# First node pass of a graph network: one inverse root for two norms, normalised rows written by ScalarE

## The reference, cut to what matters

```python
def _layernorm(x, axis=-1, eps=1e-05):
    m = jnp.mean(x, axis=axis, keepdims=True)
    v = jnp.var(x, axis=axis, keepdims=True)
    return (x - m) / jnp.sqrt(v + eps)
...
h = x @ w_in + b_in                                   # x is _layernorm of the input
...
xn = _layernorm(h, ln1_g[l], ln1_b[l])                # l = 0
q = (xn @ wq[l] + bq[l]).reshape(n, H, DH)
k = (xn @ wk[l] + bk[l]).reshape(n, H, DH)
v = (xn @ wv[l] + bv[l]).reshape(n, H, DH)
```

## Time and profile before

| what | us |
|---|---|
| median of 3 runs | 4462.18 |
| lowest and highest run | 4457.46, 4467.36 |
| span of the profiled execution, from its first to its last instruction | 4465.3 |
| TensorE busy in it | 3681.2 (82%) |
| VectorE busy in it | 3232.5 (72%) |
| ScalarE busy in it | 1681.1 (38%) |
| POOL busy in it | 2072.2 (46%) |

### The profile page before, as it was taken

How to read it: one execution, slowest core, us unless ns; L and a number is a source line. 1 busy time by engine, 2 the same in 40 slices (tenths; PEclk the granted TensorE clock), 3 DMA queues, 4 the chain that set the end, 5 groups by cost and what they waited for, 6 DMA issues and landing times. The chain is left out here.

```text
span 4465.3 us, 82525 instructions
## 1 busy us (share of the span) xinstructions
PE 3681.2 (82%) x17048; PEld 2435.5 (55%) x17048; DVE 3232.5 (72%) x7299; ACT 1681.1 (38%) x4755; POOL 2072.2 (46%) x1938
## 2 busy tenths in 40 slices
PE   1777898888998857999988888888888758888488
PEld 1444555555555535777765555455555437777377
DVE  4777899888998865555548998898899766666501
ACT  0111555555555521222214555555555402222021
POOL 2113777777777730000007777777777500000022
PEclk8998999999999978999999999999999979999699
DMA  4224777777777731111117777777777512222011
GB/s 73 85 87 134 214 218 216 212 212 214 218 221 213 219 108 33 48 59 59 59 49 219 217 213 211 207 218 214 213 217 219 170 48 71 82 74 83 23 47 39
DMA packets 357834, 640.43 MB, mean 143 GB/s; under 512 B 107755, under 2 KB 199981, under 8 KB 357594
## 3 DMA queue, kind: packets, MB, share of 16 engines
q0 software_dynamic: 140144, 457.44, 34.7%
q1 hardware_dynamic: 217610, 182.03, 13.9%
HBM read 570.14 MB, written 69.95 MB: 143 GB/s over the span
## 5 line engine op out<-in xcount | busy, mean ns | idle before, releaser
L673 POOL DMA_INDIRECT edge_kv<-kv,edge_idx x1664 | 1871.0, 1124 | 542.1 <-issue 423.0
L852 PE MATMUL edge_sums<-edge_kv,edge_sel 128*128 128x272 f32 x3328 | 979.2, 417 | 142.0 <-ACT edge_sums L920 112.4
L805 PE MATMUL edge_q<-qc,edge_spread 128*128 x3328 | 921.3, 400 | 155.4 <-DVE edge_kv L715 130.4
L919 ACT COPY acc<-edge_sums x1664 | 641.2, 385 | 868.6 <-PE edge_sums L852 704.5
L805 PEld LDWEIGHTS edge_q<-qc,edge_spread 128*128 128x128 f32 x3328 | 580.6, 192 | 430.1 <-issue 374.6
L852 PEld LDWEIGHTS edge_sums<-edge_kv,edge_sel 128*128 128x128 f32 x3328 | 566.6, 190 | 441.8 <-issue 364.2
L715 DVE TENSOR_TENSOR edge_kv<-edge_kv,edge_q 128x512 f32<-128x512 f32 x832 | 564.7, 679 | 242.8 <-DMA edge_kv<-kv,edge_idx 227.2
L920 ACT COPY edge_sums<-edge_blank 128x272 f32 x1664 | 659.6, 396 | 0.0
L764 DVE TENSOR_TENSOR edge_kv<-edge_kv 128x512 f32<-128x512 f32 x832 | 564.4, 678 | 0.9 <-ACT edge_kv L909 0.9
L722 DVE TENSOR_REDUCE edge_score<-edge_kv 128x16 f32<-128x512 f32 x832 | 559.4, 672 | 0.2
L758 DVE TENSOR_TENSOR edge_sel<-cols,edge_tab 128x256 f32<-128x256 f32 x832 | 340.4, 409 | 0.0
(11 more groups left out here) (367 smaller groups left out, 3974.8 us busy)
## 6 DMA issues: line engine op xcount, KB each, us to landing
edge_rel<-step_rel SPq DMA_DIRECT2D x208, 256.0 KB
edge_kv<-kv,edge_idx POOLq DMA_INDIRECT x1664, 3.8
edge_flags<-step_flags SPq DMA_DIRECT2D x416, 32.0 KB
picked<-last_picked SPq DMA_DIRECT2D x25, 513.0 KB
kv<-first_kv_out SPq DMA_DIRECT2D x25, 512.0 KB
kv<-middle_kv_out SPq DMA_DIRECT2D x25, 512.0 KB
end_rows<-edge_ends SPq DMA_DIRECT2D x416, 8.5 KB
h<-first_h SPq DMA_DIRECT2D x25, 256.0 KB
```

The lines of the kernel that those rows point to most:

```text
L673: nc.gpsimd.indirect_dma_start(kv[:, turn[0], j, 0:KV], None, dram["kv"], bass.IndirectOffsetOnAxis(ap=idx[:, turn[0], j:j + 1], axis=0)). ...
L805: mm = t.matmul(psq[m % QBUFS][:, j % 2, :], spread[:, turn[0] % 2, j * P:(j + 1) * P], qc[:, bass.ds(at[j % 2], D)], start=True, stop=True)
L852: pe_p.tick(t.matmul(psa[:, bass.ds(place[j % 2], QC)], sel[:, j, :], kv[:, turn[0], j, D:ROW], start=False, stop=True, skip_group_check=T ...
L919: s.copy(acc[:, bass.ds(at, QC)], psa[:, bass.ds(bank, QC)])
```

## The change

The diff adds a function `first_pass` and calls it for the first pass in place of `node_pass`. The two other node passes still use `node_pass`.

- VectorE's body now is: statistics of x (turn b); h of turn b−1; moments of x; statistics and moments of h; then `var` and `minus_half` once for all four blocks (two of x of turn b, two of h of turn b−1; tiles of four columns, two lanes); the biases of block 0 of turn b−2 (`kv0`, `q0`); wait for POOL's power; `square`, `scaled`, `newton` once for four columns; a new step `shift` = −mean times root; the biases of block 1 (`kv1`, `q1`), `qk` and `self` of turn b−2.
- POOL's power works on four columns once per body.
- The normalised rows are written by ScalarE as `Identity(scale * row + bias)` with `scale` = the root and `bias` = `shift`, both per-partition pointers: two blocks of x into `xn`, two of h into `hn`. Then ScalarE copies the transposed x and applies gain and bias to the transposed h.
- TensorE's body now is: transposes of x (turn b), transposes of h (turn b−1), product with w_in (turn b), QKV product (turn b−1). The transposes have a PSUM tile each, `pt_x` and `pt_h`.
- SP loads x once ScalarE has normalised the turn two before.

The core of the diff:

```diff
+def first_pass(nc, a, dram, keep, weights):
...
+        def _(sp):
...
+                if not first:
+                    act_x.wait(sp, later(turn, -2), f"normed{W - 1}", beside=s_zero)
...
+        def _(pool):
...
+                    dve_root.wait(pool, turn, "var", beside=s_zero)
+                    pool_root.tick(nc.gpsimd.tensor_tensor(rs[:, i, of], var[:, i, of], power[:, of], ALU.pow),
+                                   turn, "guess")
...
+        def _(dve):
...
+                if exists(turn):
+                    landed(dve, s_x, turn)
+                    stats(dve_x, turn, i, x[:, i, :, :], 0)
+                if exists(old):
...
+                    pe_x.wait(dve, old, "projected")
+                    dve_h.tick(v.tensor_tensor(h[:, old[0], :, :], pp[old[0]][:, :].rearrange("p (w d) -> p w d", w=W),
+                                               each(b_in[:, :]), ALU.add), old, "h")
+                if exists(turn):
+                    moments(dve_x, turn, i, 0)
+                if exists(old):
+                    dve_h.wait(dve, old, "h")
+                    stats(dve_h, old, i, h[:, old[0], :, :], W)
+                    moments(dve_h, old, i, W)
...
+                    dve_root.tick(v.tensor_scalar(var[:, i, of], mv[:, i, of, 1], EPS, None, ALU.add), turn, "var")
...
+                if exists(older):
+                    stored_before(dve, s_kvout, older)
+                    values(older, 0)
+                if root:
+                    pool_root.wait(dve, turn, "guess")
...
+                    dve_root.tick(v.scalar_tensor_tensor(out=shift[:, i, of], in0=mv[:, i, of, 0], scalar=-1.0,
+                                                         in1=rs[:, i, of], op0=ALU.mult, op1=ALU.mult), turn, "shift")
+                if exists(older):
+                    values(older, 1)
...
+        def _(pe):
...
+                if exists(turn):
+                    act_x.wait(pe, turn, f"normed{W - 1}")
+                    turned(pe_x, turn, xn, pt_x)
+                if exists(old):
+                    act_h.wait(pe, old, f"normed{W - 1}")
+                    turned(pe_h, old, hn, pt_h)
+                if exists(turn):
...
+                    act_x.wait(pe, turn, "copied")
...
+                if exists(old):
+                    act_h.wait(pe, old, "scaled1")
...
+        def _(act):
...
+                    told.tick(s.activation(into[:, w, :], rows[:, w, :], ACT.Identity, bias=shift[:, i, at + w:at + w + 1],
+                                           scale=rs[:, i, at + w:at + w + 1]), turn, f"normed{w}")
...
+                    dve_root.wait(act, turn, "shift")
...
+                    act_x.tick(s.copy(xt[:, :], pt_x[:, :]), turn, "copied")
...
-            node_pass(nc, "first", a, dram, keep, Weights(nc, held, "first", a, keep))
+            first_pass(nc, a, dram, keep, Weights(nc, held, "first", a, keep))
```

231 lines of the change are left out of this document (added).

## The result

The changed kernel takes 4418.88 us (median of 4 runs, 4415.88 to 4424.01) against 4464.77 us of the kernel before in the same comparison: a ratio of 0.989, 95% interval 0.9868 to 0.9913. In a later comparison the same two kernels gave 0.9878 (0.9849 to 0.9906); one run of the changed kernel that took 7275.97 us, far from the 4397 to 4422 of its five others, is left out of that ratio. The forecast was 4412 with a range of 4393 to 4440.

A forecast was written before the change was run, and what follows sets the result against it. VectorE's order was taken to bound the first node pass; after the change, a one-turn loop. Head 11.0, 24 turns of 9.4 (225.6), slow clock 3.0 and tail 15.6 make 255.2 against 305.85: 50.6 less, 4411.6 us, range 4393 to 4440.

The forecast's parts named there:

- VectorE's order: First node pass before the change: VectorE's instruction order sets the turn, 11.81 and 12.38 us alternately, 12.10 on average.
- The loop: Product of turn b waits, through h, root, ScalarE and transposes, for that of turn b−1: about 9.4 us, 4412, chance 0.70.
- R: End of the product of turn b−1 on TensorE, from which the loop's terms are counted.
- square: Root's first small step on VectorE, after `kv0` and `q0`: starts 3.7 us after product b−1 ends, POOL's power hidden.
- end of `shift`: VectorE's last step before ScalarE's blocks: ends 4.46 us after product b−1 ends.
- end of ScalarE's blocks: Four normalised blocks on ScalarE, about 2.1 us together: done 6.6 us after product b−1 ends.
- next R: End of the next turn's product on TensorE: 9.25 us after the previous one, 9.35 with the register-arithmetic waits.
- waits with register arithmetic: Two waits in the loop, each estimated to add some 0.05 us, taking 9.25 to 9.35.
- the slow clock in the first turns: TensorE's slow clock in the first two turns of the pass: 3.0 us added to the sum.
- The head: Start of the pass, from 96.69 to the first product's end: 11.0 us, including table load and half clock after idleness.
- the tail: End of the pass after the 24 turns, from the last root and blocks to the last additions: 15.6 us.
- second and fourth rival: TensorE's clock falls every second turn, 4432, chance 0.14; or one-turn loop at half clock throughout, 4560, chance 0.05.

## Why the prediction was right

**What bounded the pass before.** VectorE's order, as forecast: the new order alone, with all of VectorE's normalising and both roots kept, takes 1.7 us off a turn, and there VectorE waits for no other engine but POOL, once a turn and not twice. That run changes TensorE's order too; no run changes VectorE's alone.

**The loop.** It was called the likeliest case from the diff, and the runs bear it out: an addition in it moved the turn by 0.49, a shorter way by −0.32, an addition outside it by nothing, and where VectorE's own work is made longer than the loop, VectorE stops waiting for h. Its terms, in the turn above, from R at 207.51 (the product ahead of it starts at 205.54 and takes 1.97), forecast and measured: h 0.1 and 0.04; square 3.7 and 3.56; end of `shift` 4.46 and 4.30; end of ScalarE's blocks 6.6 and 6.50; next R 9.35 and 9.01. No term is off by more than 0.2: the end of `shift` came 0.16 sooner, nearly all of it ahead of the square, the product follows the start of h's transposes by 0.49 and not by the 0.66 of the whole group, and the 0.1 for waits with register arithmetic was not there.

**The prices without a row.** ScalarE's blocks and POOL's power of four columns, grouped by form over the whole changed kernel:

```profile
L2019 ACT ACTIVATE first_xn<-first_x,first_shift,first_rs 128x256 f32<-128x256 f32 x50 | 27.3, 593 | 128.1 <-DVE first_shift L1946 128.1
L2019 ACT ACTIVATE first_hn<-first_h,first_shift,first_rs 128x256 f32<-128x256 f32 x50 | 27.0, 587 | 5.2 <-DVE first_shift L1946 5.2
...
L2019 ACT ACT_TABLE_LOAD x1 | 1.3, 1283 | 99.1 <-DVE first_shift L1946 99.1
```

```profile
L1877 POOL TENSOR_TENSOR first_rs<-first_var,first_power 128x4 f32<-128x4 f32 x24 | 24.2, 1006 | 196.8 <-DVE first_minus_half L1931 196.8
```

600 ns was the estimate for a block, and the table is loaded once. The power takes 1006 ns against the 690 of two columns, 0.3 more than its cover was worked out with; `kv0` and `q0` had 0.5 to spare and still hide it, with 0.3 left.

**Where the sum was off.** The pass is 11 us shorter than forecast (96.07 to 340.22 = 244.2 against 255.2): 24 turns of 9.03 instead of 9.4 are 8.9, and the slow clock in the first turns cost about 1.3 instead of 3.0 (the second product ends 10.35 after the first, all later turns are at 9). The head, 10.8, was forecast as 11.0, the tail, 15.3, as 15.6. So two of the signs that the prediction gave for being right did not come: product ends 9.3 to 9.5 apart, and the last sum of the pass near 352. Part of the 9.4 was a branch of 0.57 every second turn on VectorE, which no longer appears. These 11 us are then hidden in the whole by the 8.5 us of the last node pass and the edge passes' scatter, so that 4418.88 lies above 4412 and not below it. That the forecast of the whole came so near is in part luck: two errors of opposite sign.

**The slower clock** of the second and fourth rival did not come: all QKV products of the pass take 5.32 to 5.43, and the clock of the pass rose to 0.96.

**The rule of the Trainium skill** that I set aside, page "ScalarE: Activation LUTs", section "Rules for kernel authors" (plain additions and multiplications on VectorE, not on ScalarE), held for this change: blocks on VectorE make the pass 15.3 us shorter. By the rule 13 us were worked out as an estimate, from the two engines' prices; that the two numbers are near says little, for the run that shows 15.3 ended at TensorE's own work. And with a root for each norm the same move to ScalarE made the pass 22.9 us shorter, against the rule: there VectorE's own work set the turn. My reason for setting it aside, that VectorE has no idle time, was read from the kernel before; in the changed kernel it waits 2 us a turn, by the loop that the prediction itself described. I named the loop and did not ask what the moved work costs inside it.

## What to carry to other kernels

When two chains are merged to save instructions, look for what one of them now waits on: a shared step, or the order of an engine's queue, makes a loop between turns, and while that loop is longer than any engine's own work only its length counts, on busy and idle engines alike. Take work out of the loop, even into a new wait, before moving it to an engine with idle time; and price a moved operation in the waits of the kernel after, not of the kernel before. Judge a stage by its own length in the profile: here the stage moved by 61 us, and the whole by 46.

## What the runs showed of the hardware that was not expected

- The end of VectorE's loop iteration cost 0.57 us in the kernel before, where the last instruction is awaited by its own engine. In the run with the new order alone, where VectorE again sets the turn and nothing waits for the last sum, turns alternate between 10.16 and 10.23 us (transposes of h at 201.46, 211.62 and 221.85; products with w_in, 10.16 and 10.24): a branch behind an instruction that nobody awaits costs about 0.1. This is argued from comparing these kernels; no run changes that wait alone.
- POOL's power took 690 ns for two columns and 1006 ns for four, some 160 ns for a column.
- In the middle of the last node pass the granted clock fell below 1.00 in some profiles and not in others, with TensorE busy 86 to 87 of 100 us in both; each profile in which it fell has a last pass 5 to 10 us longer than the kernel before.
